# Attention and a mixture of experts on one core: the last block's key and value stores moved behind two barriers, and six unused products on TensorE before attention

## The reference, cut to what matters

```
Q = (content @ Wq).reshape(b, n, HEADS, HEAD_DIM)      # K and V likewise
scores = jnp.einsum('bqhd,bkhd->bhqk', Q, K) / math.sqrt(HEAD_DIM)
alpha = jax.nn.softmax(scores, axis=-1)                 # over all keys
alpha = jnp.where(causal, alpha, 0)                     # cut after the softmax
Y = jnp.einsum('bhqk,bkhd->bqhd', alpha, V)
x = _layernorm(x + Y)
x = _layernorm(x + ffn(x))                              # router, 8 experts, top 2
```

## Time and profile before

| | |
|---|---|
| median of 3 runs | 1752.76 us |
| the profiled execution, its own time | 1756.82 us |
| its span, first to last instruction | 1755.1 us |
| PE busy | 1637.6 us (93%) |
| ACT busy | 1260.0 us (72%) |
| DVE busy | 1145.5 us (65%) |
| mean granted clock of TensorE | 0.974 of full speed |

### The profile page before, as it was taken

The page is one execution under the profiler, slowest core; times in us unless marked ns, Lnnn a source line. Parts: engine busy times, 40 slices in busy tenths (PEclk is TensorE's granted clock), DMA queues, the critical chain, the costliest instruction groups (busy, mean ns, idle before and its releaser), DMA issues. The chain is left out here.

```text
span 1755.1 us, 31201 instructions
## 1 busy us (share of the span) xinstructions
PE 1637.6 (93%) x12802; PEld 952.7 (54%) x12802; DVE 1145.5 (65%) x1767; ACT 1260.0 (72%) x1356; POOL 276.6 (16%) x230
## 2 busy tenths in 40 slices
PE   8989999999999999999999964599999999999996
PEld 6723333333333333333333322588989998899985
DVE  7847777777877777778777766545454444544475
ACT  7879999999999999999999963424243332432333
POOL 1000000000000000000000000233332515335144
PEclk9979999999999999999999987799999999999998
DMA  7794060420601505106010016022222414324043
GB/s 257 248 155 119 11 77 1 51 37 1 87 1 20 68 1 66 21 1 86 1 49 1 1 40 225 23 61 75 47 78 50 110 37 90 75 49 110 10 132 119
DMA packets 78895, 118.26 MB, mean 67 GB/s; under 512 B 9202, under 2 KB 62811, under 8 KB 78734
## 3 DMA queue, kind: packets, MB, share of 16 engines
q1 hardware_dynamic: 63840, 98.32, 24.2%
q0 software_dynamic: 14880, 17.82, 5.7%
q10 hardware_dynamic: 32, 0.07, 0.0%
HBM read 80.22 MB, written 40.37 MB: 69 GB/s over the span
## 5 line engine op out<-in xcount | busy, mean ns | idle before, releaser
L860 DVE TENSOR_REDUCE sums<-expq 128x1 f32<-128x1536 f32 (+7 forms) x576 | 559.0, 1033 | 187.6 <-ACT expq L833 187.3
L833 ACT ACTIVATE probs<-scores 128x1536 f32<-128x1536 f32 (+1 forms) x384 | 509.9, 1480 | 13.5 <-PE scores L749 13.5
L833 ACT ACTIVATE expq<-scores 128x1536 f32<-128x1536 f32 x320 | 447.3, 1536 | 2.2 <-PE scores L749 0.6
L769 PE MATMUL o_ps<-probs,v 128*32 128x256 f32 (+1 forms) x4864 | 349.5, 369 | 1.0 <-issue 1.0
L749 PE MATMUL scores<-aq,ak 98*128 98x512 bf16 (+3 forms) x1280 | 305.9, 354 | 10.1 <-PEq L596 6.7
L1517 ACT ACTIVATE gate<-up_ps 128x512 f32<-128x512 f32 x128 | 76.6, 598 | 323.1 <-PE up_ps L1331 311.5
L749 PE MATMUL scores<-ak,aq 98*128 98x512 bf16 (+3 forms) x1184 | 265.1, 343 | 22.6 <-ACT probs L833 16.9
L749 PEld LDWEIGHTS scores<-aq,ak 98*128 98x128 bf16 x1280 | 95.4, 98 | 215.4 <-ACT expq L833 76.2
L1331 PE MATMUL up_ps<-xeT_hi,wup_hi 128*128 128x512 f32 x512 | 203.0, 396 | 1.9 <-DVE xeT_lo L1749 1.4
L1331 PE MATMUL up_ps<-xeT_lo,wup_hi 128*128 128x512 f32 x512 | 202.2, 395 | 0.0
L1845 DVE TENSOR_TENSOR mid<-up_ps,gate 128x512 f32<-128x512 f32 x128 | 88.3, 690 | 174.1 <-ACT gate L1517 167.6
(11 more groups left out here) (244 smaller groups left out, 1906.8 us busy)
## 6 DMA issues: line engine op xcount, KB each, us to landing
raw<-w_T SPq DMA_DIRECT2D x16, 1024.0 KB, 7.1
split_dram<-parts SPq DMA_DIRECT2D x48, 256.0 KB, 2.9
aq<-split_dram SPq DMA_DIRECT2D x42, 256.0 KB
ak<-split_dram SPq DMA_DIRECT2D x42, 256.0 KB
raw<-wg_T SPq DMA_DIRECT2D x8, 1024.0 KB, 4.9
v_dram<-vst SPq DMA_DIRECT2D x8, 544.0 KB, 4.7
v<-v_dram SPq DMA_DIRECT2D x8, 544.0 KB, 24.0
xT<-x_T SPq DMA_DIRECT2D x8, 512.0 KB, 5.7
```

The source lines that it names most:

```text
L769: last = nc.tensor.matmul(o_ps[g % O_RING][32 * h:32 * h + 32, col:col + w], value(gg, k, h, 32), probs[:, m % 2 * GH + h, at:at + w], sta ...
L833: nc.scalar.activation(dst, src[:, 0:w], ACT.Exp, scale=HD ** -0.5).then_inc(exp_done, 1)
L860: last = nc.vector.tensor_reduce(sums[:, gg % 2, col, h:h + 1], expq[:, at % X_RING, lo:lo + w], AX.X, ALU.add)
```

## The change

The stores of a block become two helpers, `store_parts` (three DMAs) and `store_values` (one DMA). For block 7 part 1 issues only the three stores of queries. The three stores of keys and the store of values stand at the head of SyncE's list in attention, ahead of `load_columns`; in the loose case, where it applies, they are issued in part 2, on a semaphore of their own. (In the loose case the list of attention would issue them again; it is not taken here.)

TensorE gets three products at the end of part 1's list and three in part 2, behind the load of `flag` and ahead of the branch. Each multiplies `ident` (128 x 128, float32) with `after` (128 x 512, float32) into PSUM. Nobody reads the results, and they signal nothing.

```diff
+WARM = (3, 3)
...
+            def store_parts(sp, n, i, done):
+                b, cols = n // NG, slice(n % NG * BLK, (n % NG + 1) * BLK)
+                sp.wait_ge(proj_split, U + U * n + DC * (i + 1))
+                for s in range(3):
+                    sp.dma_start(split_dram[i, s, b * D:(b + 1) * D, cols].rearrange("(c p) t -> p c t", p=P),
+                                 parts[:, s, DC * i:DC * (i + 1), cols]).then_inc(done, 16)
+
+            def store_values(sp, n, done):
+                b, at = n // NG, n % NG * 4 * VW
+                sp.wait_ge(v_read, 4 + 4 * (n + 1))
+                sp.dma_start(v_dram[b * GPB:(b + 1) * GPB, :, at:at + 4 * VW].rearrange("g p c -> p g c"),
+                             vst[:, n % NG].rearrange("p g t c -> p g (t c)")).then_inc(done, 16)
...
+                    store_parts(sp, n, 0, parts_stored[n % NG])
+                    if n + 1 < NB:
+                        store_parts(sp, n, 1, parts_stored[n % NG])
+                        store_values(sp, n, parts_stored[n % NG])
...
                 nc.tensor.matmul(proj[0:1, 0, 0:H], top[:], ident[0:H, 0:H], start=True, stop=True).then_inc(top_row, 1)
+                for n in range(WARM[0]):
+                    nc.tensor.matmul(proj[:, 1, :], ident[:], after[:].rearrange("p r k -> p (r k)"), start=True, stop=True)
...
                 loose = pe.value_load(flag[0:1, 0:1], min_val=0, max_val=1)
+                for n in range(WARM[1]):
+                    nc.tensor.matmul(m_ps[:], ident[:], after[:].rearrange("p r k -> p (r k)"), start=True, stop=True)
...
             @block.sync
             def _(sp):
+                store_parts(sp, NB - 1, 1, parts_stored[NG - 1])
+                store_values(sp, NB - 1, parts_stored[NG - 1])
                 load_columns(sp, aq[0], ak[0], slice(1, GH), slice(BLK, N), a_loaded[1])
```

More of the change, by code:

```diff
@@ L593, in program @@
         g_loaded, g_link, g_scores, g_read = sem("g_loaded"), sem("g_link"), sem("g_scores"), sem("g_read")
-        g_max, g_row, g_row_sb, g_stored, g_over = sem("g_max"), sem("g_row"), sem("g_row_sb"), sem("g_stored"), sem("g_over")
+        g_parts, g_row, g_row_sb, g_stored, g_over = sem("g_parts"), sem("g_row"), sem("g_row_sb"), sem("g_stored"), sem("g_over")
         g_again = sem("g_again")
@@ L607, in _ @@
                 with sp.If(loose > 0):
-                    for n in range(NG):
+                    store_parts(sp, NB - 1, 1, g_parts)
+                    store_values(sp, NB - 1, g_parts)
+                    for n in range(NG - 1):
                         sp.wait_ge(parts_stored[n], 16 * 7 * B)
+                    sp.wait_ge(parts_stored[NG - 1], 16 * (7 * (B - 1) + 3))
+                    sp.wait_ge(g_parts, 16 * 4)
                     sp.wait_ge(none_stored, 16 * B)
```

## The result

The changed kernel takes 1759.93 us (median of 10 runs, 1756.78 to 1764.49), the kernel before 1752.98 us (10 runs, 1751.67 to 1755.76). The ratio is 1.0036, 95% interval 1.0028 to 1.0044: slower by 0.28 to 0.44%, 4.9 to 7.7 us. The prediction was 1757.3 us, +4.5 us (its own range 3.3 to 5.6). A second comparison on another chip gave 1.0032 (1.0020 to 1.0044), 3.5 to 7.7 us.

The account below looks back on a forecast made before the run. The prediction took attention's exponentials as the bound, held up by the first loads' landing. +1.3 us (part 2, first barrier included) and +3.2 us (stores ahead of loads) gave +4.5 us on 1752.76: 1757.3 us, range 1756.1 to 1758.4.

Parts of the forecast that it names:

- The bound: Attention: the exponentials bound it, and their first uninterrupted stretch waits on loads landing at 108.6 us, ahead of slot 8.
- The first barrier: After part 1: TensorE's drain over three products ends it at 90.2 us instead of 91.1, 0.9 us earlier.
- rival 2: At the barriers: products don't hold the drains, first barrier 2.3 us earlier, total 1753.7 us, no tellable change; chance 0.08.
- Part 2: Between part 1 and attention: flag load and three products delay SyncE's first issue in attention from 93.87 to 95.15, +1.3 us.
- Four stores ahead of the loads: Head of SyncE's attention list: 3.8 us of store data delay the loads, net +3.2 us, ends 2.3 and 3.8.
- The dense start: Attention's loads: queued behind the stores they start dense instead of thin, giving back 0.6 us.
- the clock's return: Behind slot 8: TensorE needs 5.7 us to regain full clock, and the gapless exponentials begin after 7.4 us, as before.
- a sum of 3.6: Attention's loads: if their reads begin under the stores' writes, the store term tends to 2.3 and the sum to 3.6.
- The clock: TensorE in attention: full at the first slot, half again at slot 8 after some 7 us idle, so worth nothing.
- rival 1: Attention: the clock stays full through slot 8's wait, change costs 2.1 us, total 1754.9 us; chance 0.12.
- rival 3: Between the two sets of products: the clock drops, second set takes 5.3 us, +7.1, total 1759.9 us; chance 0.12.
- The total: Whole kernel: +4.5 us, 1757.3 us, own range 3.3 to 5.6; chance 0.58.

Follow-up runs that it names:

- e4_behind: The changed kernel with attention's twelve loads first in SyncE's list and the four moved stores behind them; ratio to the kernel before 1.0056.
- e3_products: The changed kernel with the stores put back in part 1, so only the six products are added; ratio to the kernel before 1.0017.
- e6_heads: The kernel before with attention's first loads in two groups, head 1 (slot 8 waits), then heads 2 and 3 (slot 9 waits); ratio 0.9987.
- e8_before_again: The kernel before, unchanged, run again as a control; ratio 0.9997.
- e9_three: The kernel before with attention's first loads head by head in three groups, 36 DMAs, each waited for ahead of its slot; ratio 1.0009.
- e5_by_act: The changed kernel with the four moved stores issued by ScalarE in part 2 instead of by SyncE in attention; ratio to the kernel before 0.9999.
- e7_all: e5_by_act and e6_heads together, with three products in part 1 and only one in part 2; ratio to the kernel before 0.9989.
- e2_moved: The changed kernel with the four stores moved but none of the six products; ratio to the kernel before 1.0017.
- e12_act_only: e5_by_act without any of the six products, loads in the order of the kernel before; ratio to the kernel before 0.9995.

## Why the prediction was right, and where its sizes were off

**The bound.** Right. The loads' landing is what attention's first slots wait for, in the kernel before and in every variant but e4_behind, where it is the value store's. Slot 11 and the end of attention keep their distance.

**The first barrier.** Right: TensorE's drain is the last, 3.0 us after the mark, as forecast (90.2 - 87.24), and rival 2, products that don't hold the drains, is out.

**Part 2.** Forecast +1.3 us for SP's start, measured 7.26 - 6.63 = +0.6. The products took 2.84 us as worked out (2.74 and 0.1). What was mis-sized is the flag's load, taken at the 1.20 us of before; it took 0.49. It took 0.49 or 0.50 in all nine kernels whose stores are moved, where the DMA engines carry little at that moment, and 1.15 to 1.19 in e3_products, e6_heads, e8_before_again and e9_three, where part 1's stores still fill them. The products alone don't change it. That the full engines slow it is the likely reason; no run had one without the other.

**Four stores ahead of the loads.** The sign and mechanism are shown by e5_by_act, the size was too small: +3.2 forecast, 19.27 - 14.73 = +4.5 measured from SP's start to slot 8 in the changed kernel. By the second table 4.1 us of it lie ahead of the loads' first packet, which is the stores' own part, and 0.7 behind their last. That last part is as long in e3_products, which has no stores ahead, so it is not the stores' doing; what sets it is open. The data were taken at 355 GB/s, 3.8 us; they ran at 310 to 313 in the windows, and 4.1 us passed between the first packet of the stores and that of the loads. The issues were cheaper than forecast, 2.0 us for the four (93.85 to 95.87), and not the bound. The dense start did come: over the loads the DMA share is 1.04 instead of 0.95. But of the 0.6 us for it only 0.2 came, 12.9 us instead of 13.1 from first to last, because a packet of the loads took 353 ns on average instead of 335. The two errors, -0.7 in part 2 and +1.3 here, cancel in part: slot 8 is +5.2 us from the mark, where 4.5 was forecast. That it came so close is in part luck.

Behind slot 8 the clock's return decides. Forecast were 5.7 us for it and 7.4 until slot 11, as before. In the first trace of the changed kernel it came after 3.6 us, and slot 11 after 6.5 (+4.2 from the mark); in the second after 6.6 and 7.8 (+5.7). ScalarE's wait of 0.72 us for the value store, which the forecast put at nothing, lies under slot 8's wait, as it said of such a wait.

The Trainium skill's sentence on one queue's order ("DMA: Bandwidth & Descriptors", section "Two DMAs through the same engine are not ordered"), by which the forecast saw that the loads might begin under the stores, led to a sum of 3.6. The trace does not bear this out as a gain: the first packets of the loads come 0.5 us before the last store packet ends, and the term came out above the 3.8 us of plain succession, not below.

**The clock.** Right in what mattered: full at attention's first slot, half at slot 8, nothing gained (rival 1 is out). What I had not seen is that it can fall earlier, between the products (e3_products, rival 3's mechanism in another kernel) and within the first slots (e3_products, e5_by_act, e7_all). In the changed kernel itself it held until TensorE's wait for the loads in the first trace, and fell at 102.8, ahead of slot 7, in the second. Neither cost anything, since slot 8 had yet to wait.

**The total.** +4.5 lies below the interval of the first comparison (4.9 to 7.7 us) and inside that of the second (3.5 to 7.7). At the end of attention the traces show +3.8 and +5.8. Of the first median's +7.0 us up to 1 to 3 us stay unexplained; the part behind attention scatters by as much between executions and chips, and ten runs do not resolve it.

## What to carry to other kernels

A store that is moved out of the way of a barrier still stands in a queue, and what it is put in front of pays for its data, even if its issues are cheap: look for the load that a wait ends on, and put nothing ahead of it. Products that only keep the clock up hold the drains of a barrier, and they are lost if the engine then waits longer for something else; first shorten that wait, for instance by letting the first slot wait for its own head alone (e6_heads, where it took slot 8's wait away and gained perhaps 2 us). Smaller transfers help only until their issues are the bound (e9_three).

## What the runs showed of the hardware

The same twelve loads, 144 KB each, ran at 123 (e2_moved, e3_products), 132, 135, 136, 140 (both traces of the kernel before), 151 (e4_behind) and 166 GB/s (e12_act_only), each over 7 or 8 us with the DMA share at 1.05 to 1.07 and nothing else large in the queues. Neither TensorE's clock nor whether they were queued behind the stores sorts these numbers: 123 GB/s is found with stores ahead and without. What does stays open. From their first packet to the end of their last, these loads took 11.3 us in e12_act_only, 11.6 in e4_behind, 12.9 to 13.2 in both kernels' own traces, 13.6 in e5_by_act and 13.8 in e2_moved and e3_products: a spread of 2.5 us, over half of what the stores ahead of them cost.
